# Single bank pair for the scores by key, log weights added by TensorE, and scores of the third attention by row groups

## The chip, the cores and the metric

The program runs on one core of a Trainium2 chip. The metric is the time of one execution in device microseconds. TensorE's array clock has two levels here, 1.2 and 2.4 GHz; the profile gives the granted clock as a share of 2.4 GHz (0.50 and 1.00, and means of them over a stretch).

## The reference

Four layers, each an attention and a feed-forward part with a residual, on x of 2 x 1024 tokens of 128 features, after a layer norm for each part. Only two of the eight parts are touched.

The first attention is causal with 16 heads of 8 features. To the scores a mask of -log(distance + 1) is added, which is the same as multiplying the exponentials by weights 1 / (distance + 1):

```
log_d = jnp.log(jnp.maximum(delta, 0).astype(jnp.float32) + 1.0)
mask = jnp.where(delta > 0, (-ALPHA * log_d).astype(dtype), 0)
mask = jnp.where(delta < 0, -inf, mask)
o = softmax(q k^T / sqrt(8) + mask) v
```

The third attention is linear and causal: phi(x) = elu(x) + 1 of queries and keys, 16 heads of 8 features; numerators are sums over earlier keys of (phi(q) . phi(k)) v, divided by the same sum without v. It goes through 16 blocks of 128 tokens: within a block by masked scores, before it by a running state.

## The kernel before

**First attention** (`l0_attn`, line 172). Work is cut into 8 units (2 sequences x 4 groups of 4 heads). The queries and keys of a head pair lie in two row halves of the array, rows 0 and 64 up, split into bf16 parts stacked on 48 rows (51 with the negated maxima). A unit has two passes:

- Maxima: 24 pieces (`PIECES`), each two heads by up to 512 keys. TensorE forms scores by query (`scores_by_query`, L418, and L422 adds the causal mask at 128 columns in 16 of the 24); VectorE reduces them to negated maxima (`maximum`, L578). In unit 0 three pairs of banks alternate; from unit 1 on there is one pair, banks 0 and 1. Splitting the maxima into three bf16 parts (L588 to L596), turning them (L430), a copy (L534) and a DMA put them beside the queries.
- Exponentials: 12 groups (`GROUPS`, 512 queries by 128 keys; 6 of them full, then 384, 256 and 128 wide twice in some order), each in two halves of two heads, 24 halves a unit. Per half: TensorE's scores by key (`scores_by_key`, L445, and L449 with the mask in 16 of the 24), in banks 2 and 3 or 4 and 5 alternately; one exponential of ScalarE over both heads (L522) into one of six ring buffers (buffer 0 is xnT); a multiplication by the weights (`weigh`, L372) on GpSimd or VectorE, as the planner `shares` divides them (135 and 57 of 192); and for each whole group `times_v` (L465), four float32 matmuls side by side in column groups of 32 with zero-padded values. Two banks, 6 and 7, take the numerators of the two query chunks; they are copied (L530), turned (L473) and divided (L604, L607).

`schedule` fixes the order of each engine's work by due slots, one slot a half: exp at h, then the maxima pieces of the following unit (`PIECES_AT`), VectorE's weighing at h + 2, `times_v` at about h + 7. The maxima of unit 1 are spread over the first 14 halves of unit 0; those of unit u over 24 halves that begin 10 before unit u - 1; the last 34 halves have none. TensorE's waits: a maxima piece waits for the reduction of the piece before it (`ahead`), scores by key for the exponential two halves before. Before all this all of unit 0's maxima are formed alone.

**Third attention** (`l2_attn`, line 955). `gpsimd` lays the 16 heads' queries of a block side by side, 2048 columns, each masked to its 8 rows (L1013). `scores` (L1049) multiplies by all 128 rows of keys in four float32 matmuls of 512 columns, banks 0 to 3; each waits for VectorE's causal masking (L1164) of its bank in the block before. Then come numerators of the block before (L1064, L1069), the state (L1055, masked at L1170), transposes (L1079) and a division (L1176 to L1180). Every fourth block has an output projection (L1087 to L1091, L1187) and the next layer norm's statistics. In the lead-in VectorE forms phi (L1137, L1154, L1157) while GpSimd starts on the first blocks.

A float32 matmul leaves two records in the profile, a bf16 or float32r matmul one.

## Time and profile before

| | us |
|---|---|
| median of 3 runs | 1376.7 |
| lowest, highest | 1374.12, 1377.26 |
| the profiled execution | 1373.5 |
| its span | 1371.7 |

| engine | busy us | share |
|---|---|---|
| TensorE matmul | 1130.8 | 82% |
| VectorE | 839.4 | 61% |
| GpSimd | 512.0 | 37% |
| ScalarE | 468.2 | 34% |

In the profile, PE is TensorE and PEld its weight loads, DVE is VectorE, ACT ScalarE, POOL GpSimd, SP the engine that issues DMAs. L418 is line 418. The first attention takes about the first 478 us, the third from 586 to 732. Matmul durations contain the way through the array, so two that follow each other closely overlap; what a matmul occupies is the distance between starts.

### The profile page before, as it was taken

What the parts mean: (1) busy time and instruction counts of PE and PEld (TensorE: products, weight loads), DVE (VectorE), ACT (ScalarE), POOL (GpSimd) and SP (SyncE); (2) the same over time, 40 slices, a digit from 0 to 9 for tenths busy, and PEclk for the clock granted to TensorE, in tenths of its full rate; (3) what the DMA queues carried; (4) which work ended last, traced back from release to release, by engine and by line L of the source; (5) the groups of instructions that cost most, each with busy time, mean ns of one, the idle gap of its engine ahead of it and who ended that gap; (6) DMA issues with size and microseconds to landing.
All of it is one profiled execution on the core that took longest, in us unless ns stands there. A gap on an engine that the chain in (4) does not pass through costs nothing.

```text
span 1371.7 us, 19117 instructions
## 1 busy us (share of the span) xinstructions
PE 1130.8 (82%) x7112; PEld 728.4 (53%) x7112; DVE 839.4 (61%) x1898; ACT 468.2 (34%) x765; POOL 512.0 (37%) x346
## 2 busy tenths in 40 slices
PE   4668778778778693669997999759997899999998
PEld 2212222222222352535665766549675788888887
DVE  5755666776768747785654699950366544444444
ACT  3123343444346321140112576633421422332222
POOL 5064665676667411536541588841001100000000
PEclk9556777887868897689997999969999799999999
DMA  5500000001000000010000002110000000000001
GB/s 176 148 0 22 4 24 25 1 25 24 2 1 19 16 3 6 12 47 1 1 1 1 11 21 75 39 47 1 1 0 1 0 24 23 23 23 23 23 0 31
DMA packets 23356, 31.75 MB, mean 23 GB/s; under 512 B 3578, under 2 KB 16882, under 8 KB 23158
## 3 DMA queue, kind: packets, MB, share of 16 engines
q1 hardware_dynamic: 23286, 30.81, 7.4%
q8 instruction: 44, 0.72, 0.2%
q14 instruction: 26, 0.21, 0.1%
HBM read 23.27 MB, written 7.34 MB: 22 GB/s over the span
## 4 chain that ended last, share of the span: by engine, by line
PE 61%; DVE 30%; issue 4%; ACT 2%; SPq 1%; POOL 1%; DMA 1%; DVEq 0%; POOLq 0%; ACTq 0%
DVE arena L578 10%; PE ps L1877 8%; PE ps L465 5%; PE ps L418 4%; PE ps L1854 4%; PE ps L1049 4%; PE ps L1855 4%; PE ps L1856 4%; DVE arena L372 4%; PE ps L422 2%; PE ps L1586 2%; DVE x L1457 2%; PE ps L445 2%; DVE arena L1430 1%; DVE arena L1426 1%
## 5 line engine op out<-in xcount | busy, mean ns | idle before, releaser
L578 DVE TENSOR_REDUCE arena<-ps 128x2 f32<-128x1024 f32 (+1 forms) x192 | 181.7, 956 | 126.4 <-PE ps L422 92.7
L372 POOL TENSOR_TENSOR arena<-arena 128x1024 f32<-128x1024 f32 (+3 forms) x111 | 208.1, 1892 | 98.6 <-ACT arena L522 98.4
L522 ACT ACTIVATE arena<-ps 128x1024 f32<-128x1024 f32 (+3 forms) x160 | 127.4, 810 | 179.8 <-PE ps L449 139.1
L418 PE MATMUL ps<-arena 48*128 48x512 bf16 (+3 forms) x384 | 81.9, 424 | 88.6 <-DVE arena L578 86.2
L1919 ACT ACTIVATE arena<-ps 128x512 f32<-128x512 f32 x128 | 76.2, 597 | 197.3 <-PE ps L1856 197.3
L2009 DVE TENSOR_TENSOR arena<-ps,arena 128x512 f32<-128x512 f32 x128 | 88.5, 691 | 67.3 <-PE ps L1856 60.3
L1877 PEld LDWEIGHTS ps<-arena 128*128 128x128 f32 x1024 | 118.6, 192 | 2.2
L1877 PE MATMUL ps<-arena 128*128 128x128 f32 x1024 | 118.8, 275 | 0.0
L1854 PE MATMUL ps<-rounded 128*128 128x512 f32 x256 | 103.4, 404 | 2.8 <-DVE arena L2009 2.0
L1855 PE MATMUL ps<-rounded 128*128 128x512 f32 x256 | 100.7, 393 | 0.0
L1856 PE MATMUL ps<-rounded 128*128 128x512 f32 x256 | 100.5, 393 | 0.0
L116 POOL TENSOR_SCALAR vareps<-meanvar 128x4 f32<-128x4 f32 x32 | 7.7, 241 | 228.4 <-DVE meanvar L97 228.4
L465 PE MATMUL ps<-arena 128*32 128x512 f32 (+3 forms) x640 | 88.3, 632 | 4.2 <-DVE arena L372 3.6
L372 DVE TENSOR_TENSOR arena<-arena 128x1024 f32<-128x1024 f32 (+3 forms) x49 | 88.4, 1816 | 4.8 <-ACT arena L522 4.8
L418 PEld LDWEIGHTS ps<-arena 48*128 48x128 bf16 x384 | 19.5, 98 | 132.5 <-DVE arena L578 124.6
L1997 DVE SCALAR_TENSOR_TENSOR x<-ps,arena,x 128x128 f32<-128x128 f32 x128 | 36.0, 344 | 86.5 <-PE ps L1877 86.5
L151 PE MATMUL ps<-ident,xn 128*128 128x128 f32 x128 | 26.4, 356 | 68.8 <-DVE xn L105 25.4
L445 PE MATMUL ps<-arena 51*128 51x512 bf16 (+3 forms) x384 | 75.8, 392 | 7.8 <-DMA arena<-arena 5.2
L372 POOL TENSOR_TENSOR xnT<-xnT,arena 128x1024 f32<-128x1024 f32 (+1 forms) x24 | 47.5, 1992 | 89.0 <-ACT xnT L522 89.0
L1013 POOL TENSOR_TENSOR arena<-arena 128x2048 f32<-128x2048 f32 x16 | 58.2, 3638 | 56.0 <-PE ps L1049 51.7
L1286 PEld LDWEIGHTS ps<-arena 128*128 128x128 f32 x512 | 60.9, 192 | 31.5 <-ACT arena L1340 21.1
L1286 PE MATMUL ps<-arena 128*128 128x128 f32 x512 | 64.7, 280 | 9.2 <-ACT arena L1340 9.2
(258 smaller groups left out, 2116.5 us busy)
## 6 DMA issues: line engine op xcount, KB each, us to landing
arena<-scratch SPq DMA_DIRECT2D x32, 192.0 KB, 4.1
arena<-in_L_ffn_w SPq DMA_DIRECT2D x8, 768.0 KB, 4.2
scratch<-arena SPq DMA_DIRECT2D x12, 256.0 KB, 4.4
arena<-in_L_ffn_w SPq DMA_DIRECT2D x8, 257.0 KB, 2.6
scratch<-arena SPq DMA_DIRECT2D x4, 384.0 KB, 5.3
scratch<-arena SPq DMA_DIRECT2D x12, 128.0 KB, 4.4
x<-in_x SPq DMA_DIRECT2D x4, 256.0 KB, 3.7
arena<-in_L_attn_wqkT SPq DMA_DIRECT2D x1, 1024.0 KB, 5.7
```

The lines of the kernel that those rows point to most:

```text
L372: engine.tensor_tensor(e, e, weight[:, at:at + k].unsqueeze(1).broadcast_to([P, 2, k]), ALU.mult).then_inc(done, 1)
L418: mm = nc.tensor.matmul(m.ps[:, bank + e, 0:wd], qs[rows, u % BUFS, pair, i * P:(i + 1) * P], ks[rows, u % BUFS, pair, i * P + j:i * P + j ...
L445: mm = nc.tensor.matmul(m.ps[:, 2 + 2 * p + e, 0:wd], ks[rows, u % BUFS, p, kt * P:(kt + 1) * P], qs[rows, u % BUFS, p, CH * qc:CH * qc + ...
L465: mm = nc.tensor.matmul(m.ps[PAD * h:PAD * (h + 1), 6 + qc, 0:wd], vpad[:, b * TB + kt, u % G * GH + h, :], probs(u * NG + n)[:, h, 0:wd], ...
L522: nc.scalar.activation(probs(g)[:, 2 * p:2 * p + 2, 0:wd], m.ps[:, 2 + 2 * p:4 + 2 * p, 0:wd], ACT.Exp, scale=SCALE).then_inc(exps, 1)
L578: nc.vector.tensor_reduce(negmax[:, u % 2, j // CH, 2 * pair:2 * pair + 2, i], m.ps[:, bank:bank + 2, 0:piece_width(n)], AX.X, ALU.max, ne ...
L1286: mm = nc.tensor.matmul(m.ps[:, 4 + k % 2, j * P:(j + 1) * P], hT[:, k % 2, f, j * P:(j + 1) * P], w[:, u, W2 + f * P:W2 + (f + 1) * P], s ...
L1854: nc.tensor.matmul(out, w_high[:, u, col:col + P], x_high[:, cs], start=True, stop=False)
L1855: nc.tensor.matmul(out, w_high[:, u, col:col + P], x_low[:, cs], start=False, stop=False)
L1856: return nc.tensor.matmul(out, w_low[:, u, col:col + P], x_high[:, cs], start=False, stop=True)
L1877: last = nc.tensor.matmul(m.ps[:, 4 + k % 2, j * P:(j + 1) * P], hT[:, k % 2, f, j * P:(j + 1) * P], w[:, u, W2 + f * P:W2 + (f + 1) * P], ...
L2009: nc.vector.tensor_tensor(hT[:, k % 2, f, :], m.ps[:, 2 * (s % 2) + 1, :], sg[:, s % 2, :], ALU.mult).then_inc(h_done, 1)
```

## The change

In the first attention:

- The maxima use two pairs of banks, 0 to 3, alternately, in all units (unit 0 had three pairs).
- Scores by key use banks 4 and 5, one for each head of a half. The exponential is split in two, one for each bank; the matmul of a head waits for that head's exponential in the half before. All masks and log weights of a half are issued after both heads' scores.
- VectorE weighs nothing. The planner gives GpSimd 121 halves of 192. In the other 71, TensorE adds sqrt(8) times the log of the weights to the scores before the exponential: two float32r matmuls with an identity for each head, high and low part. Both parts are made once, by ScalarE and GpSimd in turn.
- Numerators take bank 6 alone, by 9-column weights (8 features and a one) where 32 columns with zeros stood; VectorE clears the bank once. Their transposes and those of the maxima share bank 7. The copy, the transposes and the division of numerators come one slot earlier.

In the third attention GpSimd keeps four heads' columns in place of sixteen, 512: each row keeps its own head's place within its group of 32 rows (`own`, made by one VectorE reduction). The four score matmuls read 32 rows each.

```diff
+    sb("rounded", [P, 2 * S + P])
+    m.rounded.fresh()
+    log_high, log_low = (m.rounded.take(f"l0a_log_{n}", [P, S], F32R) for n in ("high", "low"))
+    identr = m.rounded.take("l0a_identr", [P, P], F32R)
...
-        by_pool, pool, dve = set(), 0.0, 0.0
+        by_pool, pool, gone = set(), 0.0, 0.0
         for h in range(UNITS * HALVES):
-            dve += sum(150 + 1.04 * 2 * piece_width(n) for _, n in PIECES_AT.get(h, ()))
-            u, n = divmod(h // 2, NG)
-            if h % HALVES == 0:
-                dve += 4000
-            k = 2 * width(n)
-            if pool + 100 + 2.45 * k <= dve + 160 + 1.2 * k:
+            k = 2 * width(h // 2 % NG)
+            gone += 1.8 * k
+            if pool <= gone:
                 by_pool.add(h)
                 pool += 100 + 2.45 * k
-            else:
...
-                    for what, late in (("take_num", 2), ("turn_num", 4), ("divide", 5)):
+                    for what, late in (("take_num", 1), ("turn_num", 3), ("divide", 4)):
...
+    def set_ones(pool):
+        nc.gpsimd.memset(vones[:, :, :, HD:HD + 1], 1.0).then_inc(v_ones, 1)
 
     def gpsimd(pool):
         pool.wait_ge(w_in, w_all)
+        pool.wait_ge(log_steps, 1)
+        nc.gpsimd.tensor_scalar(logw, weight[:, :], 1e-30, None, ALU.max).then_inc(log_steps, 1)
+        pool.wait_ge(log_steps, 3)
+        nc.gpsimd.tensor_scalar(logw, logw, 1 / SCALE, None, ALU.mult).then_inc(log_steps, 1)
+        pool.wait_ge(log_steps, 5)
+        nc.gpsimd.tensor_tensor(log_low, logw, log_high.bitcast(F32), ALU.subtract).then_inc(log_steps, 1)
         for u in range(UNITS):
             for n in range(NG):
...
-            ahead = 3 if u == 0 else 1
-            if k >= ahead:
-                pe.wait_ge(max_set, k - ahead + 1)
-            bank = 2 * (k % ahead)
+            if k >= 2:
+                pe.wait_ge(max_set, k - 1)
...
-            if h >= 2:
-                pe.wait_ge(exps, h - 1)
             wd = width(n)
             diagonal = kt // TPC == qc
+            with_log = h not in BY_POOL
             for e in range(2):
                 rows = slice(HALF * e, HALF * e + LONG)
-                mm = nc.tensor.matmul(m.ps[:, 2 + 2 * p + e, 0:wd], ks[rows, u % BUFS, p, kt * P:(kt + 1) * P],
-                                      qs[rows, u % BUFS, p, CH * qc:CH * qc + wd], start=True, stop=not diagonal, skip_group_check=True)
-            if diagonal:
-                for e in range(2):
-                    mm = nc.tensor.matmul(m.ps[:, 2 + 2 * p + e, wd - P:wd], identb[:, :], before[:, 1, :], start=False, stop=True, skip_group_check=True)
-            mm.then_inc(s_mm, 1)
+                if h:
+                    pe.wait_ge(exps, 2 * h - 1 + e)
+                mm = nc.tensor.matmul(m.ps[:, 4 + e, 0:wd], ks[rows, u % BUFS, p, kt * P:(kt + 1) * P],
+                                      qs[rows, u % BUFS, p, CH * qc:CH * qc + wd], start=True, stop=not (diagonal or with_log), skip_group_check=True)
+                if not (diagonal or with_log):
+                    mm.then_inc(s_mm, 1)
+            if with_log:
+                pe.wait_ge(log_steps, 6)
+            for e in range(2):
+                if with_log:
+                    at = weight_at(n)
+                    nc.tensor.matmul(m.ps[:, 4 + e, 0:wd], identr, log_high[:, at:at + wd], start=False, stop=False, skip_group_check=True)
+                    mm = nc.tensor.matmul(m.ps[:, 4 + e, 0:wd], identr, log_low[:, at:at + wd], start=False, stop=not diagonal, skip_group_check=True)
+                if diagonal:
+                    mm = nc.tensor.matmul(m.ps[:, 4 + e, wd - P:wd], identb[:, :], before[:, 1, :], start=False, stop=True, skip_group_check=True)
+                if diagonal or with_log:
+                    mm.then_inc(s_mm, 1)
...
-            done = POOL_COUNT[u * HALVES + 2 * n + 1]
-            pe.wait_ge(weighed_p, done)
-            pe.wait_ge(weighed_v, u * HALVES + 2 * n + 2 - done)
+            last = u * HALVES + 2 * n + 1
+            pe.wait_ge(weighed, POOL_COUNT[last])
+            if last not in BY_POOL or last - 1 not in BY_POOL:
+                pe.wait_ge(exps, 2 * (last if last not in BY_POOL else last - 1) + 2)
             if kt == TB - 1:
-                if u:
-                    pe.wait_ge(o_set, QC * (u - 1) + qc + 1)
-                if qc == 1:
-                    pe.wait_ge(mrows_set, min(u + 2, UNITS))
+                if u * QC + qc:
+                    pe.wait_ge(num_out, u * QC + qc)
+                else:
+                    pe.wait_ge(cleared, 1)
             for h in range(GH):
-                mm = nc.tensor.matmul(m.ps[PAD * h:PAD * (h + 1), 6 + qc, 0:wd], vpad[:, b * TB + kt, u % G * GH + h, :],
+                mm = nc.tensor.matmul(m.ps[PAD * h:PAD * h + HD + 1, 6, 0:wd], vones[:, b * TB + kt, u % G * GH + h, :],
                                       probs(u * NG + n)[:, h, 0:wd], start=(kt == TB - 1), stop=(n == LAST[qc]), skip_group_check=True)
...
+            if k:
+                pe.wait_ge(o_set, k)
+            pe.wait_ge(mrows_set, in_bank7["max"])
+            in_bank7["num"] += 1
             for j in range(TPC):
-                mm = nc.tensor.transpose(m.ps[:, 6 + qc, j * P:(j + 1) * P], numT[:, k % 2, j * P:(j + 1) * P], m.ident[:, :])
+                mm = nc.tensor.transpose(m.ps[:, 7, j * P:(j + 1) * P], numT[:, k % 2, j * P:(j + 1) * P], m.ident[:, :])
...
+        nc.scalar.activation(identr, m.ident[:, :], ACT.Copy).then_inc(log_steps, 1)
+        act.wait_ge(log_steps, 2)
+        nc.scalar.activation(logw, logw, ACT.Ln).then_inc(log_steps, 1)
+        act.wait_ge(log_steps, 4)
+        nc.scalar.activation(log_high, logw, ACT.Copy).then_inc(log_steps, 1)
+        act.wait_ge(log_steps, 6)
+
         def exp(u, at):
             n, p = at
             g = u * NG + n
             wd = width(n)
-            act.wait_ge(s_mm, 2 * g + p + 1)
             if g >= RING:
                 act.wait_ge(pv_mm, g - RING + 1)
-            nc.scalar.activation(probs(g)[:, 2 * p:2 * p + 2, 0:wd], m.ps[:, 2 + 2 * p:4 + 2 * p, 0:wd], ACT.Exp, scale=SCALE).then_inc(exps, 1)
+            for e in range(2):
+                act.wait_ge(s_mm, 2 * (2 * g + p) + e + 1)
+                nc.scalar.activation(probs(g)[:, 2 * p + e, 0:wd], m.ps[:, 4 + e, 0:wd], ACT.Exp, scale=SCALE).then_inc(exps, 1)
...
+        dve.wait_ge(m.ln_xnT, norm.value(NC - 1))
+        nc.vector.memset(m.ps[:, 6, :], 0.0).then_inc(cleared, 1)
...
-        def weigh_mine(u, at):
-            n, p = at
-            if u * HALVES + 2 * n + p not in BY_POOL:
-                weigh(dve, nc.vector, u, n, p, weighed_v)
-
-        do = {"max": maximum, "split": split_maxima, "weigh": weigh_mine, "divide": divide}
+        do = {"max": maximum, "split": split_maxima, "divide": divide}
...
+        pool.wait_ge(own_set, 1)
         for t in range(NT):
             c = t // TPC
             pool.wait_ge(phi_set, 2 * c + 1)
             if t >= 2:
                 pool.wait_ge(a_mm, G * (t - 1))
-            nc.gpsimd.tensor_tensor(qm[:, t % 2, :, :], phi[:, 0, t * P:(t + 1) * P].unsqueeze(1).broadcast_to([P, H, P]),
-                                    hmask[:, :].unsqueeze(2).broadcast_to([P, H, P]), ALU.mult).then_inc(qm_set, 1)
+            nc.gpsimd.tensor_tensor(qm[:, t % 2, :, :], phi[:, 0, t * P:(t + 1) * P].unsqueeze(1).broadcast_to([P, 4, P]),
+                                    own[:, :].unsqueeze(2).broadcast_to([P, 4, P]), ALU.mult).then_inc(qm_set, 1)
...
-                nc.tensor.matmul(m.ps[:, g, :], phi[:, 1, t * P:(t + 1) * P], qm[:, t % 2, 4 * g:4 * g + 4, :], start=True, stop=True).then_inc(a_mm, 1)
+                rows = slice(PAD * g, PAD * (g + 1))
+                nc.tensor.matmul(m.ps[:, g, :], phi[rows, 1, t * P:(t + 1) * P], qm[rows, t % 2, :, :], start=True, stop=True).then_inc(a_mm, 1)
...
+        dve.wait_ge(w_in, w_all)
+        nc.vector.tensor_reduce(own[:, :], hmask[:, :].rearrange("p (g j) -> p j g", j=4), AX.X, ALU.add).then_inc(own_set, 1)
```

## Rows read from the trace of the kernel before

**Rows 1.** The page's groups: line, engine, operation, count; busy us, mean ns; idle before, releaser.

```profile
L578 DVE TENSOR_REDUCE arena<-ps 128x2 f32<-128x1024 f32 (+1 forms) x192 | 181.7, 956 | 126.4 <-PE ps L422 92.7
...
L372 POOL TENSOR_TENSOR arena<-arena 128x1024 f32<-128x1024 f32 (+3 forms) x111 | 208.1, 1892 | 98.6 <-ACT arena L522 98.4
...
L372 DVE TENSOR_TENSOR arena<-arena 128x1024 f32<-128x1024 f32 (+3 forms) x49 | 88.4, 1816 | 4.8 <-ACT arena L522 4.8
```

**Rows 2.** Table by stretches: length, busy of PE, PEld, DVE, ACT, POOL, then granted clock.

```profile
66.00:116.00 50.00, 31.61 (x148) 7.46 (x152) 24.59 (x26) 13.04 (x14) 26.07 (x12) 0.50 0.00 1
216.00:266.00 50.00, 39.41 (x270) 11.68 (x268) 33.77 (x39) 20.27 (x27) 33.00 (x18) 0.74 0.06 17
416.00:466.00 50.00, 41.72 (x348) 15.51 (x348) 38.49 (x35) 28.37 (x42) 33.86 (x17) 0.90 0.04 13
640.00:700.00 60.00, 58.63 (x508) 37.90 (x506) 37.20 (x91) 6.92 (x12) 32.83 (x10) 1.00 0.01 1
```

**Rows 3.** DVE's timeline (start us, us, what): first operation of a split of maxima.

```profile
116.74 0.17 DVE L588 TENSOR_TENSOR arena<-arena 128x16 f32<-128x16 f32 x1
...
418.72 0.17 DVE L588 TENSOR_TENSOR arena<-arena 128x16 f32<-128x16 f32 x1
```

**Rows 4.** Chain of work that ended last, in order of time: start us, us, what.

```profile
65.99 1.82 DMA arena<-arena
...
463.66 1.77 PE ps L484 x16
```

**Rows 5.** Timeline of the third attention: one block, and four masks of the next.

```profile
661.35 3.60 PE L1049 MATMUL ps<-arena 128*128 128x512 f32 x8
...
664.79 1.05 PE L1064 MATMUL ps<-arena 128*128 128x128 f32 x8
...
667.57 3.60 PE L1049 MATMUL ps<-arena 128*128 128x512 f32 x8
...
670.39 2.45 DVE L1164 TENSOR_TENSOR arena<-ps,arena 128x512 f32<-128x512 f32 x4
```

**Rows 6.** PE's timeline in the last part: float32r matmuls following each other.

```profile
1300.02 0.39 PE L1856 MATMUL ps<-rounded 128*128 128x512 f32 x1
...
1300.25 0.39 PE L1854 MATMUL ps<-rounded 128*128 128x512 f32 x1
```

**Rows 7.** Timeline of all engines at full clock, two pieces of unit 2 and 3.

```profile
223.41 0.39 PE L445 MATMUL ps<-arena 51*128 51x512 bf16 x2
...
223.74 0.29 PE L449 MATMUL ps<-arena 128*128 128x128 bf16 x2
...
223.95 0.39 PE L418 MATMUL ps<-arena 48*128 48x512 bf16 x2
...
224.06 1.02 ACT L522 ACTIVATE arena<-ps 128x1024 f32<-128x1024 f32 x1 [2.30 <-PE ps L449]
...
226.21 0.85 PE L465 MATMUL ps<-arena 128*32 128x384 f32 x8
...
226.99 0.34 PE L445 MATMUL ps<-arena 51*128 51x384 bf16 x2
```

**Rows 8.** Groups with shapes kept apart, 66 to 466 us: exponentials of 512 columns.

```profile
L522 ACT ACTIVATE arena<-ps 128x512 f32<-128x512 f32 x16 | 9.5, 597 | 4.9 <-PE ps L449 4.9
```

**Rows 9.** Timeline: two exponentials, and TensorE released at their end.

```profile
430.64 1.94 ACT L522 ACTIVATE xnT<-ps 128x1024 f32<-128x1024 f32 x2 [1.33 <-PE ps L445]
...
432.63 0.10 PEld L445 LDWEIGHTS ps<-arena 51*128 51x128 bf16 x2 [0.32 <-ACT xnT L522]
```

**Rows 10.** Timeline: times_v of one group at the lower clock.

```profile
235.53 1.94 PE L465 MATMUL ps<-arena 128*32 128x512 f32 x8
```

**Rows 11.** DVE's timeline in the lead-in of the third attention.

```profile
592.05 0.43 DVE L1157 TENSOR_SCALAR arena<-arena 128x512 f32<-128x512 f32 x1
...
594.05 2.65 DVE L1154 SCALAR_TENSOR_TENSOR arena<-arena 128x512 f32<-128x512 f32 x1
...
596.74 3.72 DVE L1157 TENSOR_SCALAR arena<-arena 128x512 f32<-128x512 f32 x1
```

More of the change, by code:

```diff
@@ L220, in l0_attn @@
     a_mm, max_set, nsplit, nparts_set, n_turned, mrows_set = (sem(f"l0a_{n}") for n in ("a_mm", "max_set", "nsplit", "nparts_set", "n_turned", "mrows_set"))
-    s_mm, exps, weighed_v, weighed_p = (sem(f"l0a_{n}") for n in ("s_mm", "exps", "weighed_v", "weighed_p"))
+    s_mm, exps, weighed = (sem(f"l0a_{n}") for n in ("s_mm", "exps", "weighed"))
+    log_steps = sem("l0a_log_steps")
     pv_mm, num_out, num_turned, rec_set, o_set = (sem(f"l0a_{n}") for n in ("pv_mm", "num_out", "num_turned", "rec_set", "o_set"))
@@ L369, in weigh @@
         e = probs(u * NG + n)[:, 2 * p:2 * p + 2, 0:k]
[L370 to L377 removed]
+        at = weight_at(n)
+        pool.wait_ge(exps, 2 * h + 2)
+        nc.gpsimd.tensor_tensor(e, e, weight[:, at:at + k].unsqueeze(1).broadcast_to([P, 2, k]), ALU.mult).then_inc(weighed, 1)
+    def set_ones(pool):
+        nc.gpsimd.memset(vones[:, :, :, HD:HD + 1], 1.0).then_inc(v_ones, 1)
     def gpsimd(pool):
         pool.wait_ge(w_in, w_all)
+        pool.wait_ge(log_steps, 1)
[4 more added lines that the diff above has]
+        nc.gpsimd.tensor_tensor(log_low, logw, log_high.bitcast(F32), ALU.subtract).then_inc(log_steps, 1)
         for u in range(UNITS):
@@ L410, in scores_by_query @@
                 pe.wait_ge(stack_in[u % BUFS], STACK * (u // BUFS + 1))
-            ahead = 3 if u == 0 else 1
-            if k >= ahead:
-                pe.wait_ge(max_set, k - ahead + 1)
-            bank = 2 * (k % ahead)
+            if k >= 2:
+                pe.wait_ge(max_set, k - 1)
+            bank = 2 * (k % 2)
             wd = piece_width(n)
@@ L574, in maximum @@
             k = u * NP + n
-            ahead = 3 if u == 0 else 1
-            bank = 2 * (k % ahead)
+            bank = 2 * (k % 2)
             dve.wait_ge(a_mm, k + 1)
```

44 lines of the change are left out of this document (21 added, 23 removed).

## The prediction

> **What bounds the kernel now.** I read the groups of the page first. In the first attention VectorE does two jobs: 192 maxima (181.7 us) and 57 of the 192 weighings (49 of them in the group of 88.4 us), while GpSimd does the other 135 by the planner's count [rows 1]. The page also gives VectorE 126.4 us of idling before its maxima, 92.7 of them until TensorE's L422: with one pair of banks for maxima after unit 0, TensorE fills, VectorE reduces, TensorE fills again. The table by stretches comes next [rows 2]: TensorE's granted clock is 0.50 of 2.4 GHz in the first 50 us of the unit loop, 0.74 in the middle, 0.90 in the last 50 us, and 1.00 in the third attention, where TensorE is busy 58.6 of 60 us. VectorE's timeline marks the end of each unit's maxima: 116.74 for unit 1 and 418.72 for unit 7, six periods of 50.3 us [rows 3]. The rows of maxima for unit 0 land at 67.8 us (65.99 + 1.82), about 68.5 with the first scores, and the output projection begins at 463.66 [rows 4]. So the loop is 48 us (14 half groups, with 24 maxima pieces among them) + 6 x 50.3 + 45 us (34 half groups without maxima) = 395 us. The first two terms are bound by the VectorE and TensorE exchange, the last by weighing. The third attention is bound by TensorE: one block takes from 661.35 to 667.57, 6.22 us, 3.44 of them the four score matmuls (661.35 to 664.79) [rows 5].
>
> **Removed in the first attention.** All 57 VectorE weighings go, more than the 88.4 us of busy time of the group shown. GpSimd keeps 121 of 192 by the new planner (count of `shares`), about 15 a unit. At 2.4 to 2.5 us for a full one [rows 1] and less for narrow ones that is some 30 us a unit, so GpSimd is not the bound while a unit takes over 35. VectorE keeps 23 us of maxima a unit and about 2.5 us of splits and divisions: not the bound either. The second pair for maxima lets TensorE fill while VectorE reduces, so most of the 126 us of alternation goes.
>
> **Added.** (a) Log weights for 71 half groups: 284 matmuls. By the schedule a unit has about 9 such halves with 11,000 columns. A float32r matmul of 512 columns starts 0.23 us after the one before at full clock (1300.02 to 1300.25) [rows 6]; narrow ones, held by their weight loads, I put at 0.11. That is 5.6 us a unit, and 1 to 2 more for changes between the 64-row tiles and full-height matmuls: 0.32 us from the start of a 512-column L445 to the L449 after it [rows 7], when 0.21 us of columns are streamed. (b) ScalarE's exponential splits into two per half. 1024 columns take 1.02 us [rows 7], 512 take 0.597 [rows 8], so 256 some 0.385 by that slope; 192 more instructions at 0.17 us are 33 us of busy time, 4 a unit, and 26 us a unit is no bound in itself. (c) The point that decides: scores of a half now pass through banks 4 and 5 alone, where two pairs alternated. The matmul of head e must wait for the exponential of head e of the half before.
>
> **The exchange through the one pair, at full clock.** Let E be the end of a half's second exponential. TensorE starts 0.05 us after it (432.58 to 432.63) [rows 9]. In a half with the mask, mask matmuls begin 0.32 us later, end 0.29 us after that, and ScalarE starts 0.04 later (224.06 from 223.74 + 0.29) [rows 7]. Both heads' first matmuls stand ahead of the masks in the program, so the first exponential of this half also waits for the second of the half before. Two exponentials follow, the second overlapping by 0.1 (two of 1.02 us take 1.94) [rows 9]. At 512 columns E moves by 0.70 + 1.1 = 1.8 us; at 384, 256 and 128 by 1.5, 1.25 and 1.0. A half without mask or log weights moves E by 1.1 us, if TensorE is back in time. It isn't in every second half: times_v occupies TensorE for 0.78 us at 384 columns (226.21 to 226.99) [rows 7] and so about 1.0 at 512, and a masked maxima piece for 0.54 (0.33 + 0.21, as L445 and L449). Two unmasked halves with two pieces and one times_v come to 3.35 us. A log half adds 1.0 us at 512 unmasked, 0.2 to 0.45 masked. A unit is then: eight unmasked halves 4 x 3.35 + 2 x 1.0 = 15.4; the sixteen masked 2 x (3.9 + 3.3 + 2.8 + 2.1) = 24.2; logs in them 1.9; numerators and maxima through one bank each, copies and transposes not hidden, 2.4: 43.9 us. Without maxima pieces it is 38.6. At 1.2 GHz, with 1.94 us for a times_v [rows 10] and column times doubled, the same sum gives 64.
>
> Which clock? TensorE would be occupied some 38 of 44 us, more than now. The stretch where it is busy 58.6 of 60 has 1.00; the last stretch of this loop, in which it no longer alternates with VectorE, has 0.90 [rows 2]. I take nearly full clock: 44.7 us a unit, so 6 x (44.7 - 50.3) = -34. The first 14 halves carry 24 pieces, sum 29 us at full clock; they begin at the low one, so 34 us against 48: -14. The last 34 halves have nothing to hide the exchange: 38.6 + 15.2 = 54 us at full clock, 56.5 with some at the low one, against 45: +11.5. The last term is a loss because both weighing engines kept up with the two pairs there. Unit 0's maxima with two pairs in place of three, and the memset of bank 6 ahead of them: +1.5. The steps that make the log weights, with any table load they bring, lie beside the 21 us of unit 0's maxima, in which ScalarE and GpSimd are idle: 0, or up to 10 us if that cover were gone. The large memset at the start goes, but TensorE waits there for the last of its weight DMAs, so that gives 0. The 9-column weights in place of 32: 0 if four heads still run side by side, as the 48-row operands do in 64-row tiles.
>
> The Trainium skill (TensorEngine Tiling, Key Properties) says that changing the tiling mode, not the tile, drains TensorE. The row above agrees in direction, 0.1 us a change; the change adds such switches in log halves and third attention, and they are in the sum only by that row.
>
> **Third attention.** Four K=32 matmuls at rows 0, 32, 64 and 96 replace four K=128 ones. If they run side by side they take 0.86 us in place of 3.44, and TensorE's block is 3.64. No row shows row groups in float32, but the first attention's four heads in column groups take about 1.0 us together at 512 by the 0.78 at 384 [rows 7]. VectorE then has 2.45 us of masks [rows 5] and about 1.2 us of the rest, 3.7. With the handovers between them I take 4.4 us: 16 x (4.4 - 6.22) = -29. Bounds: 3.7 (-40) and 6.22 (0). GpSimd's product shrinks from 2048 columns to 512. In the lead-in the first two of them stand beside VectorE operations of 2.65 and 3.72 us [rows 11]; the like of the second takes 0.43 just before, and the first, over the same columns, some 0.7. With short ones I take back 4.5 us of the 5.2.
>
> The Trainium skill (TensorE: Matmul & The Clock Gate, Part 3) gives 3.07 times for four 32-row tiles at 512 columns, not four. By it the scores would take 1.12 us, the block 0.26 more, and the sum 4 us more. No run here shows it yet.
>
> **Sum.** The profiled execution took 1373.5 us, its span 1371.7. 1.5 - 14 - 34 + 11.5 - 4.5 - 29 = -68.5, so 1305. The median of the three runs, 1376.7, lies 3.2 above the profiled one; halfway between, I say 1307.
>
> **Rivals.** (1) TensorE alone is the bound: its occupation without waits is 38 us a unit, the ends of the exchange overlap better than I sum, and the last stretch costs nothing: 6 x -6 and -8 more, -44: 1263 to 1275. For it: waits here are short. Against: program order forbids the overlap in 16 of 24 halves. Chance 0.13. (2) The exchange is dearer and eats the first attention's gain, unit about 50 us, last stretch +14: only the third attention gains, 1340 to 1350. For it: each added semaphore wait is 0.05 us and sits on the chain. Chance 0.16. (3) The row groups don't do what they say: with a wait and an increment for each of the four, each float32 matmul's two records stay in order and only neighbours overlap, 5 x 0.43 = 2.15 us for scores, block 5.2: +13, so 1320; or no overlap at all, +29: 1336. Chance 0.12. (4) Slower: the exchange leaves TensorE waiting in every half, the clock stays at 1.2 GHz through the loop as in 66 to 116 us [rows 2], a unit takes 64 us: 6 x 13.7 + 2 + 30 - 33.5 = +80: 1455. It decides from a unit of some 54 us up, where the loop's loss exceeds the third attention's 33.5. Chance 0.05. The Trainium skill (TensorE: Matmul & The Clock Gate, A second HAM failure mode) tells of such micro-idling between groups while PSUM banks cycle. No row shows it for this order. A smaller one on that side: 9-column weights lose the side-by-side run, times_v fourfold, +28 us a unit; 0.02.
>
> **How the numbers follow.** Forecast 0.52, by itself 1285 to 1330. The range over (1), (2) and (3): 1270 to 1350. A measurement here can tell about 0.2%, 2.8 us. Faster 0.92, same 0.01, slower 0.07.
>
> **What would show it.** Right: no VectorE rows of weighing, six periods near 45 us, idle before L445 and before the exponentials ended by each other, about 54 us after the last split, clock over 0.9 in the loop; four L1049 pairs within about 1 us, blocks near 4.4 us, no VectorE row over 1.5 us near 595. Wrong: maxima still followed by idling for L422, L1049 in steps of 0.43 us, a clock of 0.5 in mid-loop, L465 in four separate starts.

## The result, and the profile after

The changed kernel takes 1335.4 us (median of four runs, 1334.8 to 1339.4) against 1376.3 for the one before in the same session: ratio 0.971, 95% interval 0.969 to 0.973, a gain of 41 us. The forecast was 1307, a gain of 69; the measured time lies outside the 1285 to 1330 of the forecast by itself and inside the wide range of 1270 to 1350. The profiled execution took 1335.8 us, its span 1334.0. One of the runs of `order` below and one of the kernel before took longer at a lower clock than the others, and the ratios leave those two out.

First the page's groups that answer to [rows 1]: line, engine, operation, count; busy us, mean ns; idle before, releaser.

```profile
L613 DVE TENSOR_REDUCE arena<-ps 128x2 f32<-128x1024 f32 (+1 forms) x192 | 179.7, 957 | 149.4 <-PE ps L428 119.4
L375 POOL TENSOR_TENSOR arena<-arena 128x1024 f32<-128x1024 f32 (+3 forms) x97 | 192.5, 2000 | 100.5 <-ACT arena L554 100.5
L554 ACT ACTIVATE arena<-ps 128x512 f32<-128x512 f32 (+3 forms) x320 | 142.6, 488 | 154.7 <-PE ps L467 117.6
L455 PEld LDWEIGHTS ps<-arena 51*128 51x128 bf16 x384 | 28.0, 94 | 136.3 <-ACT arena L554 84.2
```

VectorE's weighings are gone, yet its maxima idle longer than before (149 us against 126): it waits because a unit is now paced by something else. The last two rows name it: exponentials wait for TensorE's masks (L467), and the score matmuls (L455) wait for exponentials.

The table by stretches answers to [rows 2] (length; busy of PE, PEld, DVE, ACT, POOL; granted clock as the third number from the end, before DMA's share and rate).

```profile
66.00:107.00 41.00, 32.70 (x176) 11.11 (x176) 22.91 (x27) 16.55 (x30) 21.13 (x10) 0.65 0.00 1
107.00:153.00 46.00, 41.70 (x316) 17.03 (x308) 25.46 (x35) 23.24 (x51) 29.94 (x16) 1.00 0.08 19
199.00:244.00 45.00, 41.38 (x316) 17.03 (x308) 25.38 (x34) 23.21 (x51) 29.78 (x16) 1.00 0.08 19
347.00:375.00 28.00, 26.05 (x121) 9.09 (x120) 10.95 (x13) 10.96 (x24) 14.39 (x8) 0.51 0.00 1
389.00:452.00 63.00, 54.17 (x360) 22.97 (x356) 3.06 (x11) 31.53 (x73) 38.45 (x21) 0.89 0.04 11
```

TensorE is busy nine tenths of a unit, and in five of six units it has 2.4 GHz for nearly all of it. From 347 to 375 us it has 1.2, in one unit that is otherwise like the others.

The span splits at these instructions (a split of maxima is the work on a unit's maxima once all are reduced, see the kernel before): the first operation of each split of maxima (L623, which was L588), the output projection's first transpose (L508, was L484), and the third attention's first score matmul (L1082, was L1049). The timeline of VectorE has the splits of units 1 and 7 (the one of unit 0 is at 65.5 us), and TensorE's the transpose:

```profile
107.05 0.62 DVE L623 TENSOR_TENSOR arena<-arena 128x16 f32<-128x16 f32 x1
...
388.59 0.82 DVE L623 TENSOR_TENSOR arena<-arena 128x16 f32<-128x16 f32 x1
...
452.60 1.94 PE L508 MATMUL ps<-ident,xn 128*128 128x128 f32 x16
```

The same splits in the traces of all kernels of this study, in us. The second column runs from the split of unit 0 to that of unit 1, so it holds also the some 8 us until unit 0's first scores; "its loop" ends with the start of the last matmul of the third attention's output projection (L1124, 690.6 us). Kernels other than the first two are described under the experiments.

| kernel | to first split | first 14 halves | units 2 to 7 | last 34 halves | to third attention | its loop | rest |
|---|---|---|---|---|---|---|---|
| before | 60.3 | 56.4 | 51.4 50.8 50.7 48.5 49.9 50.8 | 44.8 | 154.1 | 111.6 | 642.4 |
| after | 65.5 | 41.6 | 45.6 46.4 44.9 45.3 44.9 54.4 | 64.0 | 152.7 | 85.3 | 643.3 |
| third_only | 61.4 | 56.4 | 50.9 48.9 50.4 48.4 50.2 48.6 | 45.8 | 152.8 | 83.1 | 642.8 |
| first_only | 66.4 | 39.5 | 45.6 45.1 48.8 45.3 44.9 45.3 | 73.6 | 158.0 | 111.6 | 644.6 |
| tail | 66.4 | 42.6 | 45.6 46.4 44.9 45.3 44.9 54.4 | 45.6 | 150.6 | 85.3 | 643.3 |
| order | 65.4 | 46.1 | 47.6 47.2 47.5 47.6 47.5 47.6 | 63.4 | 148.9 | 83.1 | 644.4 |
| no_logs | 64.8 | 36.7 | 47.4 43.7 44.3 44.4 44.3 44.4 | 60.6 | 152.9 | 83.4 | 642.8 |
| no_logs_fill | 66.0 | 48.7 | 45.1 44.9 44.9 44.9 44.9 44.9 | 62.9 | 152.8 | 85.3 | 643.4 |
| by_vector | 66.5 | 41.6 | 48.1 48.1 48.0 56.3 46.1 44.4 | 60.8 | 150.6 | 83.0 | 642.2 |
| share | 66.8 | 37.2 | 44.5 44.9 44.9 43.4 48.5 43.7 | 67.6 | 152.8 | 83.0 | 644.2 |
| tail_unit0 | 61.6 | 39.5 | 45.6 48.7 48.9 45.3 44.9 45.3 | 45.6 | 152.9 | 83.3 | 644.5 |
| best_share | 61.6 | 37.1 | 44.5 44.9 44.8 42.2 53.0 43.7 | 53.4 | 152.9 | 83.3 | 642.7 |
| best_fill | 62.6 | 48.4 | 47.4 47.6 47.7 47.3 47.9 47.7 | 53.5 | 150.7 | 83.0 | 644.2 |

Before against after, term by term: +5.2, -14.8, -20.6, +19.2, -1.4, -26.3, +0.9, together -37.7 of span. The first attention as a whole (first four columns) gave only 11 us, where the forecast's four terms came to -35. The columns are of one execution each; where its time is far from the median of its kernel, the text says so.

The third attention (TensorE's timeline of one block, then VectorE's masks after it; start us, length, what), to be laid beside [rows 5]:

```profile
639.88 1.14 PE L1082 MATMUL ps<-arena 32*128 32x512 f32 x8
640.96 1.16 PE L1097 MATMUL ps<-arena 128*128 128x128 f32 x8
642.04 1.08 PE L1102 MATMUL ps<-arena 128*32 128x128 f32 x32
643.05 0.52 PE L1088 MATMUL ps<-arena 128*128 128x144 f32 x2
643.41 0.60 PE L1112 MATMUL ps<-ident,arena 128*128 128x128 f32 x4
643.94 1.14 PE L1082 MATMUL ps<-arena 32*128 32x512 f32 x8
...
641.11 2.48 DVE L1200 TENSOR_TENSOR arena<-ps,arena 128x512 f32<-128x512 f32 x4 [2.62 <-PE ps L1082]
```

The four matmuls (eight records) run side by side: 1.08 us until L1097 starts, where they took 3.44. The block is 4.06 us, where it was 6.22.

### The profile page after: what moved, and what is told of

It is laid out like the page before. It is cut to its first block, busy times and chain, and to the rows that moved or that the text cites. A ratio compares the mean times of both kernels' runs of the same rounds, so it can differ in the third digit from the quotient of the medians.

```text
span 1334.0 us, 19810 instructions
## 1 busy us (share of the span) xinstructions
PE 1145.4 (86%) x7396; PEld 763.2 (57%) x7396; DVE 745.6 (56%) x1843; ACT 493.4 (37%) x962; POOL 456.7 (34%) x334
## 4 chain that ended last, share of the span: by engine, by line
PE 67%; DVE 19%; ACT 7%; issue 4%; SPq 1%; DMA 1%; POOL 0%; DVEq 0%; POOLq 0%; ACTq 0%
PE ps L1913 9%; PE ps L485 5%; PE ps L455 5%; ACT arena L554 4%; PE ps L1890 4%; PE ps L1891 4%; PE ps L1892 4%; PE ps L424 3%; PE ps L464 3%; DVE arena L613 2%; PE ps L1622 2%; DVE x L1493 2%; PE ps L428 2%; PE ps L1082 2%; PE ps L467 2%
## 5 line engine op out<-in xcount | busy, mean ns | idle before, releaser
L375 POOL TENSOR_TENSOR arena<-arena 128x1024 f32<-128x1024 f32 (+3 forms) x97 | 192.5, 2000 | 100.5 <-ACT arena L554 100.5
L554 ACT ACTIVATE arena<-ps 128x512 f32<-128x512 f32 (+3 forms) x320 | 142.6, 488 | 154.7 <-PE ps L467 117.6
L455 PE MATMUL ps<-arena 51*128 51x512 bf16 (+3 forms) x384 | 101.0, 356 | 32.9 <-ACT arena L554 14.9
L455 PEld LDWEIGHTS ps<-arena 51*128 51x128 bf16 x384 | 28.0, 94 | 136.3 <-ACT arena L554 84.2
L424 PE MATMUL ps<-arena 48*128 48x512 bf16 (+3 forms) x384 | 77.0, 375 | 17.6 <-DVE arena L613 16.2
L151 PE MATMUL ps<-ident,xn 128*128 128x128 f32 x128 | 26.6, 358 | 70.4 <-DVE xn L105 26.4
L485 PE MATMUL ps<-arena 128*9 128x512 f32 (+3 forms) x640 | 69.4, 511 | 0.0
L1368 ACT ACTIVATE arena<-arena 128x128 f32<-128x128 f32 x128 | 52.7, 482 | 39.8 <-DVE arena L1483 39.8
L375 POOL TENSOR_TENSOR xnT<-xnT,arena 128x1024 f32<-128x1024 f32 (+1 forms) x24 | 47.7, 2003 | 57.6 <-ACT xnT L554 57.6
L1310 PE MATMUL ps<-xnT,arena 128*128 128x512 f32 x128 | 64.2, 628 | 0.4 <-DVE arena L1441 0.4
```

The lines of the kernel that those rows point to most:

```text
L375: nc.gpsimd.tensor_tensor(e, e, weight[:, at:at + k].unsqueeze(1).broadcast_to([P, 2, k]), ALU.mult).then_inc(weighed, 1)
L424: mm = nc.tensor.matmul(m.ps[:, bank + e, 0:wd], qs[rows, u % BUFS, pair, i * P:(i + 1) * P], ks[rows, u % BUFS, pair, i * P + j:i * P + j ...
L455: mm = nc.tensor.matmul(m.ps[:, 4 + e, 0:wd], ks[rows, u % BUFS, p, kt * P:(kt + 1) * P], qs[rows, u % BUFS, p, CH * qc:CH * qc + wd], sta ...
L485: mm = nc.tensor.matmul(m.ps[PAD * h:PAD * h + HD + 1, 6, 0:wd], vones[:, b * TB + kt, u % G * GH + h, :], probs(u * NG + n)[:, h, 0:wd], ...
L554: nc.scalar.activation(probs(g)[:, 2 * p + e, 0:wd], m.ps[:, 4 + e, 0:wd], ACT.Exp, scale=SCALE).then_inc(exps, 1)
```

## Experiments

**One half of the change at a time.** `third_only` is the kernel before with `l2_attn` of the changed one; `first_only` is it with `l0_attn` of the changed one.

> The kernel before with the change of the third attention alone (GpSimd's narrow product and the scores by row groups). Theory: the two parts add up, and this one is worth 30 us (25 in the block loop, 5 in its lead-in), so about 1346. Rival: the parts act on each other through the clock; then this run and the one with the first attention alone do not add to 41 us.

Measured: 1344.6 us, ratio 0.978 (0.975 to 0.981), a gain of 29.4 us.

> The kernel before with the change of the first attention alone. Theory: 11 us gained, about 1365: 15 from the first 14 halves, 20 from the six units, less 5 in the maxima of unit 0 and 19 in the last 34 halves. Rival: the low clock in one unit and at the end of the profiled run is chance; then it gains 20 or more in the median, 1356.

Measured: 1369.2 us, ratio 0.995 (0.992 to 0.998), a gain of 4.7 us, less than the 11 expected. The third attention carries most of the gain. The two parts add to 34 us and the whole gained 41; the difference is about as large as the three intervals allow together (4 us or so each), so whether the parts act on each other is left open. In the first attention the 44 us gained in the first 14 halves and six units are nearly all given back: 6 us before them, 29 in the last stretch, 4 in the stages that follow and 2 in the rest. The last stretch is longer here than in the changed kernel, 73.6 us against 64.0, with its clock down to 0.72. A spell at 1.2 GHz as long as the one that the changed kernel has from 347 to 375 us lies inside it here (second row):

```profile
390.00:464.00 74.00, 63.72 (x352) 27.97 (x352) 8.66 (x38) 29.85 (x68) 37.33 (x23) 0.72 0.03 9
407.00:435.00 28.00, 26.35 (x103) 9.19 (x102) 0.55 (x2) 8.94 (x21) 13.87 (x7) 0.51 0.00 1
```

**The last stretch.** After the last piece of maxima banks 0 to 3 are idle. Odd halves get banks 0 and 1 for their scores, so that two pairs alternate again:

```diff
+    def score_bank(h):
+        return 0 if h > ALL_MAXIMA and h % 2 else 4
...
-                if h:
-                    pe.wait_ge(exps, 2 * h - 1 + e)
+                if h == ALL_MAXIMA + 1:
+                    pe.wait_ge(max_set, NP * UNITS)
+                elif h:
+                    pe.wait_ge(exps, 2 * h - (1 if h <= ALL_MAXIMA else 3) + e)
```

> The changed kernel, but after the last maxima piece odd halves take their scores through banks 0 and 1, which are free by then, so that two pairs alternate again as before. Theory: the last stretch (64 us) loses its 19 us because of the one pair; with two it takes 44 to 48, so 16 to 20 us less, about 1317. Rival: the low clock there or GpSimd's weighings set the 64 us; then less than 5 us are gained.

Measured: 1316.3 us, ratio 0.955 (0.951 to 0.959), as the theory said; the stretch falls from 64.0 to 45.6 us. The groups of this stretch, first of the changed kernel (389 to 452 us), then of this one (389 to 434 us):

```profile
L554 ACT ACTIVATE arena<-ps 128x512 f32<-128x512 f32 x24 | 13.0, 593 | 8.9 <-PE ps L467 6.3 <-PE ps L465 2.2 <-PE ps L455 0.3
L455 PEld LDWEIGHTS ps<-arena 51*128 51x128 bf16 x68 | 5.5, 94 | 27.8 <-ACT arena L554 21.9 <-ACT xnT L554 3.5 <-issue 1.7
```

```profile
L562 ACT ACTIVATE arena<-ps 128x512 f32<-128x512 f32 x24 | 12.5, 605 | 3.6 <-PE ps L474 3.4 <-PE ps L472 0.2
```

TensorE's score matmuls waited 25 us for exponentials through one pair, and with two pairs the exponentials' own waits shrink too. Its clock is 1.00 there. Row of the table by stretches:

```profile
389.00:434.00 45.00, 43.55 (x363) 19.35 (x366) 4.79 (x14) 30.30 (x74) 38.60 (x21) 1.00 0.05 15
```

So the one pair costs the last stretch 18.4 us. Halves 160 to 183 (numbered over all units) are at full clock in both traces, from first exponential to first exponential: 40.0 us with one pair and 28.9 with two. These 11 us are the exchange itself. The other 7 are in the rest of the stretch, where the changed kernel's clock falls as well.

**The order of the two heads.** Logs and mask of head 0 are issued before the scores of head 1, so that the first exponential can start sooner:

```diff
-            if with_log:
-                pe.wait_ge(log_steps, 6)
-            for e in range(2):
                 if with_log:
+                    if e == 0:
+                        pe.wait_ge(log_steps, 6)
```

> The changed kernel with another order in a half: the log weights and the mask of the first head are issued before the scores of the second, so the first exponential no longer waits for the second one of the half before. Theory: that program order makes the exchange dear in the 16 masked halves of a unit; by the sum of the exchange a masked half gets shorter by 0.2 to 0.5 us, a unit by some 3, the last stretch by 7: 20 to 26 us in all, about 1312. Rival: TensorE's own occupation is the bound (41 of 45 us busy by the table); then the added changes between tile heights make it the same or up to 8 us slower.

Measured: 1349.2 us, ratio 0.984 (0.978 to 0.991), slower than the changed kernel. The four runs spread from 1338.0 to 1362.7, and the profiled one is the shortest; its units take 47.5 us where they took 45. TensorE's groups of one unit, first of the changed kernel (107 to 153 us), then of this one (111.5 to 159 us):

```profile
L455 PE MATMUL ps<-arena 51*128 51x512 bf16 (+3 forms) x48 | 12.0, 333 | 3.7 <-ACT arena L554 1.8 <-ACT xnT L554 0.6
L467 PE MATMUL ps<-arena 128*128 128x128 bf16 x32 | 5.8, 227 | 0.0
```

```profile
L455 PE MATMUL ps<-arena 51*128 51x512 bf16 (+3 forms) x48 | 14.7, 333 | 2.1 <-ACT arena L550 1.3 <-ACT xnT L550 0.6
L464 PE MATMUL ps<-arena 128*128 128x128 bf16 x32 | 7.4, 230 | 0.0
```

The same instructions are busy 2.7 and 1.6 us longer. By the distance between starts, which doesn't count twice what overlaps, the score matmuls occupy TensorE 1.5 us more, the masks 1.8 and the log matmuls 0.5, in all 44.8 us of a unit where it was 41.3. Issued as a pair, the second head's score matmul starts 3 ns after the first where both are free, and a second mask 0.07 us after the first. Apart, each pays for itself, and a mask is followed by a 64-row matmul, which starts 0.15 us after it. TensorE's idling shrinks by 1.5 us only. The rival, a fuller TensorE, was right in kind.

**What the log weights cost.** `no_logs` sets `with_log = False`. `by_vector` does the same and gives the 71 half groups back to VectorE, two halves after their exponentials. `share` changes one number of the planner, `gone += 2.2 * k` for `1.8 * k`.

> The changed kernel without the matmuls that add log weights; the 71 half groups that are not GpSimd's stay unweighed, so part of the computation is left out. In a middle unit of the changed kernel TensorE is busy 41.7 of 46 us, and 12.8 of them are 36 log matmuls (7.0 and 5.8 us). Theory: TensorE's occupation is what a unit waits for, and the logs are 12.8 us of it, not 5.6 as predicted: units fall from 45.3 to 36 or 38 us (where the exchange through the one pair or GpSimd's 30 us take over), the last stretch loses about 10 us, the whole 1255 to 1275. Rival, the prediction's sum: the exchange of scores and exponentials sets the unit, and logs lie mostly beside it (1.9 us in masked halves, about 1 in others): units 42 to 43, the whole 1312 to 1320.

Measured: 1313.5 us, ratio 0.956 (0.954 to 0.959).

> The changed kernel, with the 71 half groups that are not GpSimd's weighed by VectorE two halves later, and no log matmuls; two pairs for maxima and one pair for scores stay. Tells whether the gain of the first attention comes from the second pair for maxima or from taking VectorE's weighing away. Theory: from the second pair. VectorE has 25.5 us of maxima and small work in a unit and gets about 14 more, 39 of 45; TensorE loses 12.8: units about 41, last stretch 54, the whole about 1300. Rival: VectorE's weighings stand between its maxima and keep TensorE waiting as before the change: units 45 to 50, the whole 1335 to 1365.

Measured: 1339.4 us, ratio 0.975 (0.971 to 0.979).

> One number of the changed kernel: GpSimd's allowance 2.2 in place of 1.8, so it weighs 152 half groups instead of 121 and 40 carry logs. If TensorE's occupation sets the unit: 5.5 us of logs a unit go, GpSimd is busy about 38 of it: units 41 to 42, the whole 1305 to 1312. Rival: GpSimd then finishes late, the numerators wait for it, units 45 or more, the whole 1335 to 1350.

Measured: 1332.6 us, ratio 0.970 (0.968 to 0.973).

All three miss my theory of that moment, that a unit costs what TensorE is occupied; the whole of `no_logs` and of `by_vector` came out as their rivals said, that of `share` between the two (its profiled run, 1323.4, is its shortest). The theory also had the log matmuls too dear. The 12.8 us are the busy times of two groups that overlap each other and their neighbours; by the distance between starts the 36 of them occupy TensorE 7.2 us a unit. Taking them out shortens a unit from 45 to 44.4 us, and not to the rival's 42 or 43 either. The table by stretches shows where it went: first `no_logs`, then `by_vector`, then `share`, in the same 45 us.

```profile
199.00:244.00 45.00, 39.71 (x284) 12.65 (x282) 25.60 (x34) 23.34 (x53) 30.27 (x16) 0.85 0.08 19
```

```profile
199.00:244.00 45.00, 41.18 (x259) 11.82 (x258) 34.29 (x40) 21.53 (x49) 31.73 (x15) 0.73 0.08 19
```

```profile
199.00:244.00 45.00, 40.49 (x293) 15.36 (x293) 25.66 (x34) 23.30 (x53) 36.58 (x19) 0.92 0.08 19
```

Less work on TensorE, and its granted clock falls from 1.00 to 0.85, 0.73 and 0.92, so the rest takes longer. Since every kernel issues the same halves in the same order, a unit can be compared piece by piece, from the first exponential of one half to that of the fourth after it. For unit 2 (counted from 0; in brackets the time of it at 1.2 GHz, in us):

| halves of a unit | after | no_logs | share |
|---|---|---|---|
| 0 to 3 | 6.7 | 6.1 | 6.1 |
| 4 to 7 | 10.4 (3.4) | 10.0 (6.7) | 10.6 (6.8) |
| 8 to 11 | 8.6 | 7.1 (0.1) | 8.0 |
| 12 to 15 | 7.7 | 6.8 | 7.4 |
| 16 to 19 | 7.4 | 6.6 | 6.9 |
| 20 to 23 | 6.1 | 7.7 (6.8) | 6.3 |

At full clock, halves 12 to 19 take 13.4 us without and 15.1 with their four log halves: 1.7 us for 16 matmuls, the upper end of what the forecast's exchange gave for masked log halves (0.2 to 0.45 us each). (The expectation of `no_logs_fill` below has 13.8 and 15.5 for them: these were counted from one exponential earlier. The difference is the same.) Halves 0 to 3 and 8 to 19 together, with six of the unit's nine log halves, take 26.6 us without and 30.4 with: 3.8 us for 24 matmuls that occupy TensorE 4.9 us. So at full clock most of what the log matmuls occupy comes off the unit, and the lower clock, 13.7 us of a unit at 1.2 GHz, takes nearly all of it back.

`by_vector` answers another question. With the second pair for maxima and VectorE weighing as before, the whole is within 4 us of the changed kernel. The rival's 45 to 50 us a unit was right. Its first four columns come to 460 us, before's to 464, the changed kernel's to 453. So the first 14 halves are as short with VectorE weighing as with the whole change (41.6 us in both); of the edits that are left the second pair for maxima is the likely cause, but no run has it alone. A usual unit is 48.1 us with VectorE weighing at a clock of 0.73 to 0.81 and 45 with log matmuls at 1.00. The last stretch, with the single pair for scores in both, is 16 us longer than before in this kernel and 19 in the changed one.

**Does added work bring the clock back?** From unit 1 on, ahead of each piece of maxima, one matmul whose output is overwritten:

```diff
+            if u:
+                pe.wait_ge(log_steps, 6)
+                nc.tensor.matmul(m.ps[:, bank, :], identr, log_high[:, 0:CH], start=True, stop=True, skip_group_check=True)
```

> The kernel without log matmuls (again the 71 half groups stay unweighed), with one float32r matmul of 512 columns into the first bank of a piece of maxima ahead of the piece's own matmuls, from unit 1 on: 24 a unit, 5.5 us of TensorE at full clock, whose output is overwritten. Without logs and without these, a unit took 44.4 us with a granted clock of 0.85 (13.7 us of each at 0.5); where both kernels were at full clock, eight middle half groups took 13.8 us against 15.5 with logs. Theory: the log matmuls cost the chain some 6 us a unit at full clock and pay it back by keeping the clock up; with the added work outside the chain of scores and exponentials the clock returns to 0.95 or more and a unit takes 40 to 41 us: 1285 to 1295. Rival: the clock doesn't matter to the unit, and the added matmuls cost what they last or nothing: 44.4 to 50 us a unit, 1313 to 1345.

Measured: 1325.0 us, ratio 0.964 (0.961 to 0.966), 11.6 us more than `no_logs`. Half of the theory held, the return of the clock; the times are the rival's. One unit in the table by stretches, and the added matmul's group in it:

```profile
199.00:244.00 45.00, 42.73 (x298) 15.92 (x297) 25.02 (x34) 22.66 (x51) 29.89 (x16) 1.00 0.07 19
```

```profile
L423 PE MATMUL ps<-rounded 128*128 128x512 f32 x24 | 11.7, 487 | 0.4 <-DVE arena L616 0.4
```

The clock is back at 1.00 in the units, but by the distance between starts the 24 of these occupy TensorE 10.1 us, not 5.5, and the unit takes 44.9. The profiled executions of the two kernels lie 19 us apart, and 12 of these come from the first 14 halves (48.7 us against 36.7), where the added work runs at the low clock and has twice its price (0.50 from 66 to 107 us). TensorE's timeline shows one between a mask and a 64-row matmul:

```profile
206.36 0.48 PE L423 MATMUL ps<-rounded 128*128 128x512 f32 x1
206.78 0.39 PE L427 MATMUL ps<-arena 48*128 48x512 bf16 x2
```

The next starts 0.42 us after it, where one float32r matmul follows another of its kind after 0.23 [rows 6]. Two pairs of the changed kernel tell how much of the 0.2 us is the change of tile height. After a float32r log matmul of 512 columns a 64-row matmul starts 0.33 us later, a full-height bf16 mask 0.23:

```profile
174.69 0.40 PE L465 MATMUL ps<-rounded 128*128 128x512 f32 x1
175.02 0.28 PE L424 MATMUL ps<-arena 48*128 48x256 bf16 x2
...
143.41 0.40 PE L465 MATMUL ps<-rounded 128*128 128x512 f32 x1
143.64 0.23 PE L467 MATMUL ps<-arena 128*128 128x128 bf16 x1
```

So the height costs 0.1 us here and the type nothing; the other 0.1 us of the added matmul stays open. The Trainium skill (TensorEngine Tiling, Key Properties) says that a change of the tiling mode drains TensorE; these rows agree and give a size.

**The edits together.** `tail_unit0` is `tail` with three pairs again for the maxima of unit 0. `best_share` adds `share` to it, and `best_fill` the added matmul to that.

> The kernel with a second pair of score banks after the last maximum (1316.3), with three pairs again for the maxima of unit 0. If the two pairs there cost what the difference of the first stretch says (65.5 against 61.4 us), 4 us less: 1312. Rival: the first stretch is longer for another reason (the steps that make the logs stand beside it): no change, 1316.

Measured: 1308.2 us, ratio 0.952 (0.948 to 0.955). The first stretch is 61.6 us, not 65.5: the theory held for it. The whole gained 8 us on `tail` and not 4; of the 9.5 us between the two profiled executions 4.8 are in this stretch, and the long unit of 54.4 us is absent (two of 48.7 and 48.9 stand in its place). TensorE's group in unit 0's maxima, of the changed kernel (40 to 66 us) and of this one (40 to 62 us):

```profile
L424 PE MATMUL ps<-arena 48*128 48x512 bf16 (+3 forms) x44 | 10.8, 488 | 10.0 <-DVE arena L613 10.0
```

```profile
L430 PE MATMUL ps<-arena 48*128 48x512 bf16 (+3 forms) x44 | 10.6, 478 | 6.0 <-DVE arena L622 5.5
```

> Three edits together: second pair of score banks after the last maximum, three pairs for unit 0's maxima, and 152 half groups for GpSimd. Units at full clock were 42 us with that share, but the clock fell in each of them and a unit took 43.4 to 48.5. If the gains add: 1308 less 2.7, less what a shorter last stretch gives, 1295 to 1305; if lower clock takes it all back, 1308 or more.

Measured: 1306.8 us, ratio 0.951 (0.949 to 0.953), no different from `tail_unit0` by their intervals. Five units are shorter, but one took 53.0 us and the last stretch 53.4, where `tail_unit0` has 45.6. Row of that unit:

```profile
275.00:328.00 53.00, 48.67 (x300) 17.08 (x292) 27.34 (x34) 23.27 (x51) 37.88 (x21) 0.74 0.06 16
```

> The same three edits and the matmul of 512 columns ahead of each piece of maxima from unit 1 on. Theory: the clock stays at 1.00 in the units and the added work fits in TensorE's idle 4 to 5 us: units 42 to 43, the whole 1285 to 1297, less than without it. Rival: TensorE is full, the added 5.5 us a unit lengthen it to 46 or 47: 1310 to 1320.

Measured: 1329.1 us, ratio 0.966 (0.964 to 0.968). The rival was right in kind, TensorE is full, and both missed the size: clock 1.00 in all units, and each takes 47.3 to 47.9 us. By starts TensorE is occupied 45.7 of one. Both versions of about 1307 us beat the changed kernel by 27 and 29 us. In `tail_unit0`, 22 us of that are at the end and the start of the loop; in `best_share` part of the last stretch's gain is lost to a lower clock, and the units give 8 us in its place.

## Why the prediction was right and wrong

The direction and the mechanisms came out, the size only within the wide range: the changed kernel gained 38 us of span where the terms came to 68.5. Of the 31 us that are missing, 13 are in the units, 8 in the last 34 halves, 4 each in unit 0's maxima and in the stages between, and 3 in the third loop.

- **Start, +1.5, measured +5.2.** The step "two pairs in place of three" was under-priced. With TensorE at 1.2 GHz (granted clock 0.51 from 40 to 66 us) VectorE's maxima idle 3.3 us there, and three pairs give 3.9 us back (`tail_unit0`); the log steps beside them then cost nothing that shows (61.6 us against 61.4 in `third_only`).

```profile
L613 DVE TENSOR_REDUCE arena<-ps 128x2 f32<-128x1024 f32 (+3 forms) x24 | 21.6, 950 | 3.3 <-PE ps L428 3.2
```

- **First 14 halves, -14, measured -14.8.** Right, and in its two levels too: from unit 0's first exponential to the split of unit 1 the changed kernel takes 33.4 us, where the sum had 34.
- **Units, 44.7 us each, -34.** Five took 44.9 to 46.4, so the exchange sum held as a total. It did so in part by luck. In unit 3, at full clock throughout, the eight unmasked halves took 15.1 us (15.4 in the sum) and the sixteen masked ones 30.3 (28.5, with the 2.4 for what isn't hidden). The sum's own figures for a masked half also come to 22.2 us and not to the 24.2 that it uses, and no reason is given for the 2 us more. One unit took 54.4 us, because the clock was at 0.51 for 28 us of it: +9.3, and the term became -20.6. "I take nearly full clock" is the step that failed, for that unit. Ahead of the spell TensorE was busy as in the other units (first row), and in another unit with less busy time it kept 1.00 (second row):

```profile
334.00:347.00 13.00, 12.16 (x97) 5.28 (x89) 6.91 (x10) 6.24 (x15) 6.69 (x4) 1.00 0.01 4
244.00:289.00 45.00, 40.60 (x312) 17.03 (x308) 25.14 (x33) 23.12 (x51) 29.96 (x16) 1.00 0.08 19
```

  Nothing in the trace tells why that unit and not another: `tail` has it in the same place, `first_only` in its last stretch, `best_share` in the fifth of the six units. One of the four runs of `tail` took 1306.5 us at a mean clock of 0.925, the others 1316 to 1317 at 0.912 to 0.914, so an execution of the same program may be without it; that run has no trace. What starts it stays open.
- **Log matmuls, 5.6 us a unit of TensorE, 1 to 2 more for changes of height.** Right: by the distance between starts they occupy 7.2 us. A narrow one is followed by the next after 0.16 us, not 0.11 (TensorE's timeline, a 128-column pair). What they cost the unit was taken too low: 3.8 us for six log halves at full clock, where the exchange gave 2.0 to 3.3.

```profile
244.59 0.33 PE L464 MATMUL ps<-rounded 128*128 128x128 f32 x1
244.75 0.28 PE L465 MATMUL ps<-rounded 128*128 128x128 f32 x1
```

- **Last 34 halves, +11.5, measured +19.2.** The mechanism was right and `tail` shows it. The size was not: halves 160 to 183 took 40.0 us at full clock, close to the 38.6 of the sum, but the rest of the stretch took 24.0 us and not 15.2, with TensorE at 1.2 GHz for 14 us of it (436.2 to 449.9 us). The sum put 2.5 us there for the clock.
- **Between, about 0, measured +3.6** (-1.4 with the lead-in's gain in it). Not foreseen. The code there is the same in both kernels, and `third_only`, whose first attention is that of the kernel before, has it too (from the transposes to the third attention's first projection 127.4 us, as 127.1 in the changed kernel and 123.4 before), so it doesn't come from the changed first attention. It begins in the second attention, whose granted clock is 0.67 where before it was 0.70; whether that is all of it isn't shown.
- **Lead-in, -4.5, measured -5.0.** The two long VectorE operations are gone [rows 11]:

```profile
584.17 0.69 DVE L1190 SCALAR_TENSOR_TENSOR arena<-arena 128x512 f32<-128x512 f32 x1
584.90 0.43 DVE L1193 TENSOR_SCALAR arena<-arena 128x512 f32<-128x512 f32 x1
...
586.79 1.27 DVE L1190 SCALAR_TENSOR_TENSOR arena<-arena 128x512 f32<-128x512 f32 x1
```

- **Third loop, -29, measured -26.3** (and -28.5 in `third_only`). A block is 4.06 us at full clock, better than the 4.4 taken. The loop's first 16 us ran at 0.51, where before they ran at 0.87 (rows of the changed kernel, then of the kernel before):

```profile
605.00:621.00 16.00, 15.62 (x104) 9.12 (x105) 7.98 (x14) 1.05 (x3) 6.79 (x6) 0.51 0.01 2
```

```profile
617.00:633.00 16.00, 15.37 (x92) 8.02 (x96) 8.82 (x14) 0.97 (x2) 9.86 (x5) 0.87 0.00 0
```

The Trainium skill's 3.07 times for four row tiles (TensorE: Matmul & The Clock Gate, Part 3) gave 1.12 us for the scores; the trace has 1.08, or 3.2 times, so the page was the better guide than my four.

The rivals: (1), TensorE alone as the bound, fell by 60 us; but its work is on the chain to a good part, as `no_logs` shows at full clock, and it is occupied 41.3 us of a unit, not 38. (3), row groups not side by side, had the nearest time, 1336, and that is chance: the block above shows them side by side. (2) was near in time too, but not by its mechanism: units were 45 us and not 50. (4), a clock that stays low in every unit, did not happen; a mild form of it, in one unit and at the end of the loop, accounts for some 9 us and a part of the 8 in the last stretch.

## What to carry to other kernels

Price a change of buffers where nothing else fills the gaps: the one pair for scores left units at 45 us while maxima pieces lay between, and cost 18 us where they ended, and idle banks stood ready there. Count what a matmul occupies by the distance between starts; busy times of groups that overlap made 12.8 us out of 7.2 here and led to a wrong theory. When an edit takes work off TensorE, forecast the granted clock as well as the work, and keep room in the range for a stretch at half of it; when an edit adds work to hold the clock, price it with the change of tile height on both sides. Two independent heads' matmuls that share the array must stay neighbours in the program.

## What the runs showed of the hardware beyond that

- The granted clock of a unit went from 1.00 to 0.85, 0.73 and 0.92 when log matmuls were taken out, and back to 1.00 with others put in. Busy time doesn't tell it: TensorE was busy 39.7 to 41.2 of 45 us in the three, and 40.6 in a unit of the changed kernel at 1.00.
- Four float32 matmuls of 32 rows in the four row groups took 1.08 us to the next one's start, each with a wait of its own, against 3.44 for four of 128 rows.
- After a float32r matmul of 512 columns another of its kind or a full-height bf16 mask started 0.23 us later, a 64-row matmul 0.33 us later, and 0.42 in the run with added matmuls.
- Two bf16 score matmuls in the two row halves started 3 ns apart, and a 64-row matmul 0.15 us after a mask, where a second mask started after 0.07.
